# Three rows of transfers ahead of the first norm's power, first queries on GpSimd, and experts' weights by DMA

## The chip, the cores and the metric

The kernel runs on one core of one Trainium2 chip. The metric is the device time of one execution in microseconds (us), less is better. All data is float32; large products go through TensorE as float32r parts, a high one and a low one, so that the sum keeps float32's precision.

## The reference

There are 16 images of 192 channels and 32 x 32 pixels. Three stages follow each other.

```python
x = conv_attention(x)                 # whole-image norm, per-head 1x1 and depthwise 3x3 convolutions to q, k, v,
                                      # softmax over channels, output product, residual
t = to_tokens(x)                      # 1024 tokens of 192 channels per image
t = t + causal_attention(norm(t))     # 6 heads of 32 channels, then W_proj applied twice
t = t + experts(norm(t))              # softmax gate over 4 experts, the best 2 of 4 for each token,
                                      # gelu(x @ w1[e] + b1[e]) @ w2[e] + b2[e], hidden size 768
```

In the reference the causal attention works on each image's 1024 tokens as one sequence, and each expert's answer is weighted by the token's share of the two chosen gates.

## The kernel before, in words

The kernel has two parts. The first is a loop over the images, with everything but the experts. The second is a loop over 67 blocks of 512 tokens that belong to one expert each, the experts' stage.

**An image.** TensorE makes the convolutions (`conv`, L1612), mixes the channels, and builds the image's tokens in eight chunks of 128: `input_and_first_heads(k)` (L1674) and `last_heads(k)` (L1686). VectorE takes each chunk to `t_sb` (L1004) and gathers its statistics (L964 to L971). For each half of four chunks the variances are raised to the power -1/2 by GpSimd (`token_rstd`, L695; the operation is L698), VectorE writes the normed rows `xhat` (L980), TensorE transposes them (L1696), ScalarE takes the high part and VectorE the low part (L988, L991), and TensorE makes queries, keys and values (L1713, L1721). Queries and keys are then copied inside SBUF into stacks of three parts, `QS` and `KS`, by DMAs (`load_keys`, L343; `load_queries`, L348), in three waves by token: 0 to 255, 256 to 511, 512 to 1023, and two halves j of the heads each. SP issues all keys, the queries of wave 2, and of wave 0 the half j = 0; GpSimd issues the rest of waves 0 and 1. Scores (L1752, L1754), maxima (L1010), exponentials (L1451), transposes (L1764) and products with the values (L1786, L1796) follow for 48 units. After each chunk of queries VectorE inverts the sums, GpSimd spreads them over the heads' channels (`inverse_wide`, L705; L710 and L711), and TensorE transposes that (`norms`, L1800; L1804), so that the results can be scaled.

**What GpSimd does in an image, in this order.** Every engine runs its own list of instructions in order. GpSimd's is: unpad the image (L309); send the rows of the image before; the two powers of the first norm between the sends; queries of waves 0 and 1 (`load_queries`, run at L743 to L749); two additions of the output's bias (`output_bias`, L729); and eight times the spreading of the inverse sums, with the other small powers. `send(i, first, end)` (L714) issues, for each chunk of 128 tokens (a row of the loop over k), two indirect DMAs (L723), one per chosen expert, that scatter the chunk's normed tokens to the experts' blocks in DRAM (`routed_rows`). Image 0 has nothing to send. SP waits for all sends of the image before (L551) ahead of the queries of wave 2.

**The experts' stage.** `w_all` holds all experts' weights in SBUF, high and low part. For block r GpSimd copies the expert's first layer, 128 partitions x 3072 elements, to the buffer `cur[r % 2]` in eight copies (`copy_weights`, L767; L770), two after each of the first four low parts of the block before, and the biases to `bcur` (L773). The expert's number is read from a table on the chip (`tab`). TensorE transposes the block's tokens (L1925) and runs six steps: an up product of five matmuls with `cur` (`up`, L1938; L1949), one step ahead, and a down product with `g_hi` (L1965) and `g_lo` (L1970). The first up product of a block waits for `cur_sb` (L1943). ScalarE applies gelu twice, VectorE makes the low part (L1338). SP loads the next tokens (`load_block`, L576) and stores the answers (`store_block`, L583) to DRAM. When an image's blocks are all answered, a unit of 512 tokens is fetched back by eight indirect DMAs on GpSimd (`fetch`, L779; L790), which stand between the weight copies; VectorE adds them with their shares (L1374), TensorE transposes the result (L1934), and SP stores it. There are 32 such units; `UNIT_OF` gives the block in which each is finished.

## Time and profile before

| what | value |
|---|---|
| median of 3 runs | 3534.71 us (3533.25 to 3537.79) |
| profiled execution | 3531.58 us |
| its span, first to last instruction | 3529.7 us |
| TensorE matmul busy | 3125.3 us (89%) |
| VectorE busy | 2337.5 us (66%) |
| ScalarE busy | 1836.2 us (52%) |
| GpSimd busy | 1145.8 us (32%) |
| mean granted TensorE clock | 0.959 of full speed |
| DMA | 414.50 MB, mean 117 GB/s |

PE is TensorE's matmul, PEld its weight load, DVE VectorE, ACT ScalarE, POOL GpSimd, SP the engine that issues most DMAs (SPq is its queue of DMA issues). L12 is line 12 of the kernel before. A line of a timeline gives the start and the duration in us, the engine, the line and operation, and in brackets how long the engine idled before it and what ended that. "issue" is idle time that ended with nothing the profile shows. Consecutive instructions of one kind stand in one line, with their count behind the x. The granted clock is a share of 2.4 GHz: 1.00 is 2.4 GHz, 0.50 is 1.2 GHz.

### The profile page before, as it was taken

How to read it: one execution, taken by the hardware profiler on the slowest of the kernel's cores; microseconds unless marked ns; L12 is line 12 of the kernel's file. 1: busy time of each engine (PE TensorE's matmuls, PEld its weight loads, DVE VectorE, ACT ScalarE, POOL GpSimd, SP SyncE). 2: the span in 40 equal slices, each digit the busy share in tenths (PEclk: the TensorE clock that was granted, in tenths of full speed). 3: DMA queues.
4: the chain of work that ended last, by engine and by line, in shares of the span. 5: the costliest groups of instructions: out<-in, count | busy, mean ns of one | idle time of the engine just before them, and what ended most of it. 6: DMA issues, size and time to landing. Idle time of an engine off the chain costs nothing. (4 is left out here: it accounts for less than half of the span.)

```text
span 3529.7 us, 73345 instructions
## 1 busy us (share of the span) xinstructions
PE 3125.3 (89%) x26642; PEld 2381.5 (67%) x26642; DVE 2337.5 (66%) x5867; ACT 1836.2 (52%) x3868; POOL 1145.8 (32%) x1702
## 2 busy tenths in 40 slices
PE   4899898898998989989889899866999999999995
PEld 1666666566666666666656666645888888888884
DVE  3767777677676776776767767683565665665654
ACT  0547456365474563644636547443555555555553
POOL 2131312303213133031230321303454545545554
PEclk9999999999999999999999999987999999999997
DMA  7545445444364453534644445402233333333332
GB/s 175 134 112 157 108 123 144 116 133 119 111 170 109 117 138 110 150 101 124 158 112 120 126 112 163 138 21 60 82 109 102 115 96 116 103 106 110 109 104 88
DMA packets 243804, 414.50 MB, mean 117 GB/s; under 512 B 69847, under 2 KB 156311, under 8 KB 242377
## 3 DMA queue, kind: packets, MB, share of 16 engines
q1 hardware_dynamic: 207854, 343.47, 35.9%
q0 software_dynamic: 31488, 64.53, 6.4%
q8 instruction: 217, 3.56, 0.4%
q10 hardware_dynamic: 4107, 1.81, 0.3%
q14 instruction: 138, 1.13, 0.1%
HBM read 242.82 MB, written 117.71 MB: 102 GB/s over the span
## 5 line engine op out<-in xcount | busy, mean ns | idle before, releaser
L1010 DVE TENSOR_REDUCE minus_max<-ps 128x1 f32<-128x128 f32 (+7 forms) x768 | 570.6, 749 | 228.1 <-PE ps L1754 224.3
L1451 ACT ACTIVATE p_sb<-ps,minus_max 128x128 f32<-128x128 f32 (+7 forms) x768 | 567.6, 742 | 94.0 <-DVE minus_max L1010 91.2
L1764 PE MATMUL ps<-ident,p_sb 128*128 128x128 f32 x3456 | 542.6, 282 | 42.7 <-ACT p_sb L1451 17.8
L1338 DVE TENSOR_TENSOR g_lo<-g,g_hi 128x512 fp32r<-128x512 f32 x402 | 312.5, 777 | 327.6 <-ACT g_hi L1575 327.6
L1574 ACT ACTIVATE g<-ps,bcur 128x512 f32<-128x512 f32 x402 | 276.8, 689 | 466.6 <-PE ps L1949 466.6
L1752 PE MATMUL ps<-KS,QS 96*128 96x512 f32 (+3 forms) x1152 | 404.2, 410 | 56.4 <-ACT p_sb L1451 40.5
L1764 PEld LDWEIGHTS ps<-ident,p_sb 128*128 128x128 f32 x3456 | 376.0, 143 | 96.3 <-issue 33.5
L710 POOL COPY inverse_wide<-inverse_sums 128x192 f32<-128x192 f32 x128 | 44.7, 349 | 1214.5 <-DVE inverse_sums L1031 1214.5
L1965 PE MATMUL ps<-w_all,g_hi 128*128 x1608 | 436.5, 353 | 0.0
L1465 ACT ACTIVATE PT<-ps 128x512 f32<-128x512 f32 (+3 forms) x640 | 340.8, 532 | 159.7 <-PE ps L1764 151.7
L770 POOL CAST cur<-w_all 128x384 fp32r x536 | 281.2, 557 | 392.6 <-DVE g_lo L1338 392.3
L723 POOL DMA_INDIRECT routed_rows<-xhat,slot x256 | 253.1, 989 | 372.1 <-issue 372.1
L1629 PE MATMUL ps<-ring,wconv 125*32 125x512 f32 (+1 forms) x3072 | 357.1, 605 | 18.1 <-DMA ring<-padded_scratch 18.1
L790 POOL DMA_INDIRECT got<-expert_rows,slot x256 | 254.4, 994 | 154.5 <-issue 84.8
L1949 PE MATMUL ps<-X_hi,cur 128*128 128x512 f32 x804 | 263.6, 409 | 43.1 <-issue 38.9
L1970 PE MATMUL ps<-w_all,g_lo 128*128 x1608 | 294.3, 265 | 0.0
L1023 DVE COPY PT<-ps 128x512 f32<-128x512 f32 (+3 forms) x512 | 246.7, 482 | 71.7 <-PE ps L1764 71.0
L1970 PEld LDWEIGHTS ps<-w_all,g_lo 128*128 128x128 f32 x1608 | 287.5, 189 | 4.8
L1965 PEld LDWEIGHTS ps<-w_all,g_hi 128*128 128x128 f32 x1608 | 264.9, 191 | 23.2
L1752 PEld LDWEIGHTS ps<-KS,QS 96*128 96x128 f32 x1152 | 203.0, 200 | 108.7 <-ACT p_sb L1451 60.2
L1575 ACT ACTIVATE g_hi<-ps,bcur 128x512 fp32r<-128x512 f32 x402 | 273.5, 680 | 0.0
L1949 PE MATMUL ps<-X,cur 128*128 128x512 f32 x804 | 250.9, 394 | 0.0
(279 smaller groups left out, 5663.1 us busy)
## 6 DMA issues: line engine op xcount, KB each, us to landing
ring<-padded_scratch SPq DMA_DIRECT2D x576, 204.0 KB
routed_rows<-zero_rows SPq DMA_DIRECT2D x67, 384.0 KB, 5.1
xgt<-routed_rows SPq DMA_DIRECT2D x67, 384.0 KB, 4.0
expert_rows<-y_rows SPq DMA_DIRECT2D x67, 384.0 KB, 2.6
padded_scratch<-xpad SPq DMA_DIRECT2D x32, 435.0 KB, 3.5
x_sb<-x SPq DMA_DIRECT2D x16, 768.0 KB
KS<-QKh SPq DMA_DIRECT2D x128, 96.0 KB, 2.5
KS<-QKh SPq DMA_DIRECT2D x64, 192.0 KB, 3.5
```

Source lines behind the costliest of these rows:

```text
L770: g.tensor_copy(cur[r % 2][:, part], w_all[:, bass.ds(expert, 1), part].rearrange("p e f -> p (e f)")).then_inc(cur_sb, 1)
L1010: v.tensor_reduce(nmx[:, qc, h:h + 1], score_place(n), AX, ALU.max, negate=True).then_inc(mx_sb, 1)
L1338: v.tensor_tensor(g_lo[:, n % 2, :], g32[:, n % 2, :], g_hi[:, n % 2, :].bitcast(F32), ALU.subtract).then_inc(lo_sb, 1)
L1451: a.activation(p_sb[n % NP][:, 0:P * (qc + 1)], score_place(n), ACT.Exp, bias=nmx[:, qc, h:h + 1], accum_out=ls[:, qc, h:h + 1]).then_inc( ...
L1465: a.activation(PT[h][:, k0:k0 + nb, :], bank(pass_bank(t))[:, 0:P * nb].rearrange("p (k q) -> p k q", q=P), ACT.Copy).then_inc(PT_act, 1)
L1574: a.activation(g32[:, n % 2, :], bank(n % 2), ACT.Gelu, bias=b1)
L1629: last = t.matmul(bank(2 * (r % 2) + nh)[W * j:W * (j + 1), :], wconv[s][0:KROWS[s], h, c0:c0 + W], rhs, start=s == 0, stop=s == 1, skip_g ...
L1752: t.matmul(o[:, k0:k0 + keys], QS[0:96, qc // TPC, h, P * (qc % TPC):P * (qc % TPC + 1)], KS[0:96, h, k0:k0 + keys], start=True, stop=k0 + ...
L1764: last = t.transpose(bank(pass_bank(piece))[:, P * k:P * (k + 1)], p_sb[n % NP][:, P * (k0 + k):P * (k0 + k + 1)], ident[:, :])
L1949: last = t.matmul(bank(n % 2), w[:, W1L * part + P * j:W1L * part + P * (j + 1)], act_part[:, :], start=m == 0, stop=m == 4)
L1965: t.matmul(bank(acc_bank(r, tt))[:, 0:2 * C], g_hi[:, n % 2, P * tt:P * (tt + 1)], w2j, start=j == 0, stop=False, skip_group_check=True)
L1970: last = t.matmul(bank(acc_bank(r, tt))[:, 0:C], g_lo[:, n % 2, P * tt:P * (tt + 1)], w2j[:, 0:C], start=False, stop=j == J - 1, skip_grou ...
```

## The change

On GpSimd, the sends ahead of the first power are those of three chunks (six DMAs) in place of five (ten), then two chunks' between the powers, one after the second power, and the last two chunks' (four DMAs) behind the queries of wave 0. GpSimd also issues the three query DMAs of wave 0, j = 0, that SP issued. On TensorE, `last_heads(2)` and `last_heads(3)` come ahead of `input_and_first_heads(5)`.

In the experts' stage the eight copies on GpSimd go. In their place SP issues one DMA per block from `w_all` to `cur` (`load_weights`): block 0's ahead of its wait for the sends, block r + 1's at the start of its pass r, after a wait for `up_ps`, which says that block r - 1's up products have read the same buffer. The biases are still copied by GpSimd, and the eight fetches of a unit are issued in one run, at GpSimd's pass r for a unit that is finished in block r + 2.

```diff
--- before.py
+++ after.py
@@ -286,10 +286,11 @@
         STACK_LOADS = 16 * 3
         SENT = 16 * 2 * NC
 
-        cur_sb, bcur_sb, xT_ps, xT_hi, xT_lo, up_ps, gelu_sb, lo_sb, down_ps, acc_ps, y_acc, yrow_sb = sems(
-            "cur_sb bcur_sb xT_ps xT_hi xT_lo up_ps gelu_sb lo_sb down_ps acc_ps y_acc yrow_sb")
+        bcur_sb, xT_ps, xT_hi, xT_lo, up_ps, gelu_sb, lo_sb, down_ps, acc_ps, y_acc, yrow_sb = sems(
+            "bcur_sb xT_ps xT_hi xT_lo up_ps gelu_sb lo_sb down_ps acc_ps y_acc yrow_sb")
         outT_ps, outs_sb, comb = sems("outT_ps outs_sb comb")
         xgt_ld = [sem(f"xgt_ld{n}") for n in range(3)]
+        cur_ld = [sem(f"cur_ld{n}") for n in range(2)]
         yrow_st = [sem(f"yrow_st{n}") for n in range(2)]
         got_ld = [sem(f"got_ld{n}") for n in range(2)]
         tt_ld = [sem(f"tt_ld{n}") for n in range(2)]
@@ -533,12 +534,9 @@
                 for j in range(2):
                     load_keys(sp, 0, j, 0, QKh)
                     load_keys(sp, 0, j, 1, QKh)
-                load_queries(sp, 0, 0, 0, QKh)
-                load_queries(sp, 0, 0, 2, QKh)
                 sp.wait_ge(qk_lo, NQ * i + PAIR_GROUPS)
                 for j in range(2):
                     load_keys(sp, 0, j, 2, QKl)
-                load_queries(sp, 0, 0, 1, QKl)
                 for j in range(2):
                     for r, part in enumerate((QKh, QKh, QKl)):
                         load_keys(sp, 1, j, r, part)
@@ -573,6 +571,13 @@
             sp.dma_start(tokens[B - 1], t_sb[:, :, 0:C]).then_inc(t_st, 16)
 
 
+            def load_weights(r):
+                expert = sp.value_load(tab[0:1, r:r + 1], min_val=0, max_val=E - 1)
+                if r >= 2:
+                    sp.wait_ge(up_ps, J * (r - 1))
+                sp.dma_start(cur[r % 2][:, :].bitcast(F32), w_all[:, bass.ds(expert, 1), 0:4 * W1L].rearrange("p e f -> p (e f)").bitcast(F32)
+                             ).then_inc(cur_ld[r % 2], 16)
+
             def load_block(r):
                 if r >= 3:
                     sp.wait_ge(xT_ps, 2 * (r - 2))
@@ -603,10 +608,15 @@
                 sp.dma_start(o_img[P:C, :], outs_b[u % 2][:, :]).then_inc(out_st[u % 2], 16)
 
             sp.wait_ge(t_st, 16 * B)
+            sp.wait_ge(w_split, 1)
+            sp.wait_ge(table_sb, 1)
+            load_weights(0)
             sp.wait_ge(sent, SENT * B)
             for r in range(3):
                 load_block(r)
             for r in range(NBLK):
+                if r + 1 < NBLK:
+                    load_weights(r + 1)
                 if r + 1 in UNIT_OF:
                     load_tokens(UNIT_OF[r + 1])
                 if r:
@@ -732,18 +742,22 @@
             for i in range(B):
                 unpad_image(pool, i)
                 if i:
-                    send(i - 1, 0, 5)
+                    send(i - 1, 0, 3)
                 token_rstd(i, 0)
                 if i:
-                    send(i - 1, 5, 7)
+                    send(i - 1, 3, 5)
                 token_rstd(i, 1)
                 if i:
-                    send(i - 1, 7, NC)
+                    send(i - 1, 5, 6)
                 pool.wait_ge(qk_hi, NQ * i + PAIR_GROUPS)
-                load_queries(g, 0, 1, 0, QKh)
-                load_queries(g, 0, 1, 2, QKh)
+                for j in range(2):
+                    load_queries(g, 0, j, 0, QKh)
+                    load_queries(g, 0, j, 2, QKh)
                 pool.wait_ge(qk_lo, NQ * i + PAIR_GROUPS)
-                load_queries(g, 0, 1, 1, QKl)
+                for j in range(2):
+                    load_queries(g, 0, j, 1, QKl)
+                if i:
+                    send(i - 1, 6, NC)
                 for j in range(2):
                     for r, part in enumerate((QKh, QKl, QKh)):
                         load_queries(g, 1, j, r, part)
@@ -764,19 +778,14 @@
             pool.wait_ge(t_st, 16 * B)
             pool.wait_ge(table_sb, 1)
 
-            def copy_weights(r, expert, parts):
-                for n in parts:
-                    part = slice(W1L // 2 * n, W1L // 2 * (n + 1))
-                    g.tensor_copy(cur[r % 2][:, part], w_all[:, bass.ds(expert, 1), part].rearrange("p e f -> p (e f)")
-                                  ).then_inc(cur_sb, 1)
-
-            def copy_biases(r, expert):
+            def copy_biases(r):
+                expert = pool.value_load(tab[0:1, r:r + 1], min_val=0, max_val=E - 1)
                 if r >= 2:
                     pool.wait_ge(yrow_sb, 2 * (r - 1))
                 g.tensor_copy(bcur[r % 2][:, :], wb_all[:, bass.ds(expert, 1), :].rearrange("p e f -> p (e f)")
                               ).then_inc(bcur_sb, 1)
 
-            def fetch(u, chunks):
+            def fetch(u):
 
                 i, c = UNITS[u]
                 last = last_opened(i)
@@ -784,37 +793,22 @@
                     pool.wait_ge(yrow_st[n], 16 * ((last + 2 - n) // 2))
                 if u >= 2:
                     pool.wait_ge(comb, 2 * TPC * (u - 1))
-                for kk in chunks:
+                for kk in range(TPC):
                     for a in range(2):
                         col = NC * i + TPC * c + kk
                         g.indirect_dma_start(got[u % 2][:, kk, a, :], None, answers[0:BANK * (last + 1), :],
                                              bass.IndirectOffsetOnAxis(ap=slot[:, a, col:col + 1], axis=0)
                                              ).then_inc(got_ld[u % 2], 16)
 
-            expert = pool.value_load(tab[0:1, 0:1], min_val=0, max_val=E - 1)
-            copy_weights(0, expert, range(8))
-            copy_biases(0, expert)
-            for r in range(NBLK - 1):
-                expert = pool.value_load(tab[0:1, r + 1:r + 2], min_val=0, max_val=E - 1)
-                pool.wait_ge(lo_sb, J * r + 1)
-                copy_weights(r + 1, expert, (0, 1))
-                if r + 1 in UNIT_OF:
-                    fetch(UNIT_OF[r + 1], (2,))
-                pool.wait_ge(lo_sb, J * r + 2)
-                copy_weights(r + 1, expert, (2, 3))
-                copy_biases(r + 1, expert)
-                if r + 1 in UNIT_OF:
-                    fetch(UNIT_OF[r + 1], (3,))
-                pool.wait_ge(lo_sb, J * r + 3)
-                copy_weights(r + 1, expert, (4, 5))
-                pool.wait_ge(lo_sb, J * r + 4)
-                copy_weights(r + 1, expert, (6, 7))
+            copy_biases(0)
+            for r in range(NBLK):
+                if r + 1 < NBLK:
+                    copy_biases(r + 1)
                 if r + 2 in UNIT_OF:
-                    fetch(UNIT_OF[r + 2], (0, 1))
-            assert not {NBLK, NBLK + 1} & set(UNIT_OF)
+                    fetch(UNIT_OF[r + 2])
             for u in range(len(UNITS)):
                 if finish_block(u) >= NBLK + 2:
-                    fetch(u, range(TPC))
+                    fetch(u)
 
 
         @block.vector
@@ -1852,10 +1846,10 @@
                 mixing(i, 1)
                 input_and_first_heads(i, 4)
                 pe.wait_ge(mix_sb, 2 * i + 2)
-                last_heads(i, 0)
-                last_heads(i, 1)
+                for k in range(4):
+                    last_heads(i, k)
                 input_and_first_heads(i, 5)
-                for k in range(2, 6):
+                for k in range(4, 6):
                     last_heads(i, k)
                 for k in (6, 7):
                     pe.wait_ge(y_sb, NC * i + k - 5)
@@ -1940,7 +1934,7 @@
                 if n >= 2:
                     pe.wait_ge(gelu_sb, n - 1)
                 if j == 0:
-                    pe.wait_ge(cur_sb, 8 * (r + 1))
+                    pe.wait_ge(cur_ld[r % 2], 16 * (r // 2 + 1))
                     pe.wait_ge(xT_hi, 2 * (r + 1))
                     pe.wait_ge(xT_lo, 2 * (r + 1))
                 w = cur[r % 2]
```

## Rows read from the trace of the kernel before

**Rows 1.** Waits, whole span: engine and line <- releaser: us in total, times, longest.

```profile
PE ps L1949 <- issue: 38.9, 23, 2.1
DVE xhat L980 <- POOL rstd L698: 73.6, 19, 5.6
```

**Rows 2.** Windows, images 0 and 7: us; PE, PEld, DVE, ACT, POOL busy; clock; DMA.

```profile
106.00:112.00 6.00, 3.38 (x17) 2.15 (x16) 5.30 (x18) 1.20 (x3) 0.36 (x1) 1.00 0.00 0
1107.00:1113.00 6.00, 5.79 (x17) 4.23 (x18) 4.87 (x16) 1.79 (x3) 3.93 (x4) 0.50 0.19 66
```

**Rows 3.** GpSimd's timeline in image 7; then two lines' durations, min/median/max ns.

```profile
1096.85 0.96 POOL L723 DMA_INDIRECT routed_rows<-xhat,slot  x1 [0.30 <-issue]
1101.02 0.96 POOL L723 DMA_INDIRECT routed_rows<-xhat,slot  x1 [1.95 <-issue]
1104.54 1.05 POOL L698 TENSOR_TENSOR rstd<-rstd,minus_half 128x4 f32<-128x4 f32 x1
1111.83 1.04 POOL L698 TENSOR_TENSOR rstd<-rstd,minus_half 128x4 f32<-128x4 f32 x1 [1.21 <-DVE rstd L971]
1120.88 3.72 POOL L729 TENSOR_TENSOR t_sb<-t_sb,bproj_bc 128x784 f32<-128x784 f32 x2
1131.02 0.34 POOL L710 COPY inverse_wide<-inverse_sums 128x192 f32<-128x192 f32 x1 [6.42 <-DVE inverse_sums L1031]
L723 POOL DMA_INDIRECT routed_rows<-xhat,slot x256: 954/961/1135, 233.8 to 2407.9; - x128
L351 POOL DMA_DIRECT2D QS<-QKh x96: 545/547/817, 115.0 to 2261.3; - x96
```

**Rows 4.** VectorE's timeline in image 7: start us, us, operation [idle before <-releaser].

```profile
1098.27 0.36 DVE L1004 TENSOR_TENSOR t_sb<-ps,bf_bc 128x196 f32<-128x196 f32 x1 [0.74 <-PE ps L1687]
1100.21 0.17 DVE L971 TENSOR_SCALAR rstd<-tmv 128x4 f32<-128x4 f32 x1
1105.69 1.47 DVE L980 TENSOR_SCALAR xhat<-t_sb,tmv,rstd 128x192 f32<-128x192 f32 x4 [4.65 <-POOL rstd L698]
```

**Rows 5.** TensorE's timeline in image 7.

```profile
1101.33 0.49 PE L1687 MATMUL ps<-mix,vp 128*128 128x196 f32 x2
1107.21 1.97 PE L1696 MATMUL ps<-ident,xhat 128*128 128x128 f32 x8 [5.38 <-DVE xhat L980]
1118.70 0.47 PE L1713 MATMUL ps<-T,wqkv_b_hi 128*128 128x512 f32 x1 [0.32 <-DVE T L991]
1125.46 0.30 PE L1752 MATMUL ps<-KS,QS 96*128 96x128 f32 x1 [0.43 <-DMA QS<-QKl]
1131.59 0.44 PE L1804 MATMUL ps<-ident,inverse_wide 128*128 128x128 f32 x2 [0.22 <-POOL inverse_wide L711]
```

**Rows 6.** Timeline of image 0: VectorE, then TensorE.

```profile
106.46 1.25 DVE L980 TENSOR_SCALAR xhat<-t_sb,tmv,rstd 128x192 f32<-128x192 f32 x4 [0.58 <-POOL rstd L698]
117.86 0.47 PE L1713 MATMUL ps<-T,wqkv_b_hi 128*128 128x512 f32 x1 [0.32 <-DVE T L991]
```

**Rows 7.** Timeline and one window of the experts' stage; the first is its start.

```profile
2414.47 1.09 PE L1925 MATMUL ps<-ident,xgt 128*128 128x128 f32 x4 [38.23 <-DMA xgt<-routed_rows]
2536.19 0.61 PE L1949 MATMUL ps<-X,cur 128*128 128x512 f32 x2
2525.40:2540.06 14.66, 14.66 (x88) 13.29 (x88) 7.60 (x18) 8.60 (x15) 8.00 (x13) 1.00 0.38 111
2552.03 2.31 POOL L770 CAST cur<-w_all 128x384 fp32r x4
2554.45 0.69 PE L1949 MATMUL ps<-X_hi,cur 128*128 128x512 f32 x2 [1.83 <-issue]
```

**Rows 8.** DMA issues: queue, count, KB each, median us from issue to landing.

```profile
w_raw<-w_a SPq DMA_DIRECT2D x1, 1536.0 KB, 9.8
KS<-QKh SPq DMA_DIRECT2D x128, 96.0 KB, 2.5
KS<-QKh SPq DMA_DIRECT2D x64, 192.0 KB, 3.5
```

## The prediction

> **What bounds the kernel now.** I read the list of waits first, then the windows, then the order of time around two stalls. TensorE is the engine that is busy most of the time, so I look for the places where it stands still at the same point again and again. There are two. In the list of waits [rows 1] VectorE waited 73.6 us, in 19 waits, for GpSimd's power (L698), and TensorE waited 38.9 us, in 23 waits, before an up product (L1949) for something that the view does not name.
>
> First place, image 7 (its rows stand for the 15 images that have sends; the power comes at the same point in each). GpSimd issues ten indirect sends, and only then the first power, at 1104.54 [rows 3]. What the power needs, the variances (L971), was there at 1100.21 + 0.17 = 1100.4 [rows 4]. VectorE therefore idled 4.65 us and wrote the normed rows from 1105.69 on, and TensorE idled 5.38 us before its transposes at 1107.21 [rows 4, 5]. After that idle the granted clock was 0.50, the 1.2 GHz level, for six microseconds [rows 2]. Image 0 has no sends and shows the same stretch without the stall: clock 1.00 [rows 2], and from the first normed rows to the matmul after the last low part 117.86 - 106.46 = 11.4 us [rows 6], where image 7 took 1118.70 - 1105.69 = 13.0 [rows 4, 5].
>
> Second place, the experts' stage. TensorE's up product at 2554.45 came after 1.83 us of idleness, and GpSimd's last weight copies ended at 2552.03 + 2.31 = 2554.34 [rows 7]. They were late because indirect fetches stand between the copies on GpSimd. So the unnamed wait is the one for `cur_sb`.
>
> **The change, part by part.**
> 1. *Three rows (six DMAs) ahead of the first power in place of five (ten).* The sixth send ends at 1096.85 + 0.96 = 1097.8 [rows 3]. The power then waits for VectorE and no longer for sends.
> 2. *last_heads(2) and (3) ahead of input_and_first_heads(5).* VectorE waited 0.74 us for just these [rows 4]; the variances come at 1099.5 + 0.17. The later tokens don't come later. With a power of 1.04 and two hand-overs of 0.10 (1104.54 + 1.05 to 1105.69) the normed rows start at 1100.9: 4.8 us earlier. TensorE's token work ends at 1101.8 [rows 5], so its idle time shrinks to some 0.6. Image 0, where it was busy for only 3.38 of the six microseconds, kept clock 1.00 [rows 2], so I let the slow clock go too: 13.0 - 11.4 = 1.6 more. TensorE would start the scores 6.4 us earlier, at 1119.1 in place of 1125.46 [rows 5].
> 3. *First queries.* Three query DMAs leave SP's queue, three more come onto GpSimd's, 0.547 each [rows 3]. SP's keys follow sooner. TensorE's wait there, 0.43 [rows 5], goes or stays; I take nothing.
> 4. *The last two rows (four DMAs) behind the first queries, ahead of the second ones.* Nobody waits for the sends themselves until the last queries on SP, so this is free for them. But what is queued behind them is: the second queries, two additions (L729, 3.72 us) and the spreading of the sums (L710, L711) that TensorE needs for norms. GpSimd's list from 1100.8 on is ten sends of 0.96 + 0.30 = 12.6, a power of 1.04, twelve query DMAs = 6.6, the additions 3.7, hand-overs 0.5, in sum 24.4: free at 1125.2. The eighth send shows a gap of 1.95 in place of 0.30 [rows 3]; none, one or two such gaps of 1.65 can fall in. Spreading takes 0.6, so the sums are ready between 1125.8 and 1129.1. TensorE used them at 1131.59 [rows 5] and would want them at 1131.59 - 6.4 = 1125.2. So GpSimd sets the end of this stretch: the gain is 1131.59 - 1125.8 = 5.8 at best and 1131.59 - 1129.1 = 2.5 at worst. I take one gap, 4.1 us, since the pauses before the powers cover some. What is late next is thus the first norms. Over 15 images: 62 us (37 to 87). Image 0 I take at nothing.
> 5. *Weights by one DMA per block on SP.* GpSimd's copies go, and with them the 38.9 us [rows 1]. That other work hides nothing here: in these waits TensorE had nothing else. In place comes a transfer of 128 x 3072 x 4 bytes = 1536 KB. For block r + 1, SP issues it once block r - 1 has its last up product, which frees the buffer: for the block that runs from 2540.06 that product ends at 2536.19 + 0.61 = 2536.8, and the next weights are wanted where TensorE began to wait, 2554.45 - 1.83 = 2552.6 [rows 7]. The window is 15.8 us, where a block without a stall takes 14.66 [rows 7]. The price is not in the trace. From below: 1536 KB from memory landed in 9.8 [rows 8]. From above: key loads inside SBUF took 2.5 for 96 KB and 3.5 for 192 KB, so 1.0 per 96 KB, and 3.5 + 14 x 1.0 = 17.5 [rows 8]. I take 10, the row of the same size. Behind it on SP's queue stand the answers' stores and the next tokens. With 10 the weights are in at 2546.8, 6.8 into the block, and the store, issued at 2.4, some 1 later. The fetches, now 8 in a run of 8 x 1.26 + 1.65 = 11.7, end 20 into the block, landed at 22; the first sum that needs them stands in the last step of the next block, 14.66 + 12.5 = 27 in. So 5 us of room, which hides this reordering, and which a landing of 15 would use up. First block: its transposes waited for token rows until 2414.47 [rows 7], and SP sends for the weights ahead of that wait: nothing. Sum: 39, from 20 if half the blocks with fetches stay late, to 42.
>
> Here the Trainium skill has two rules, and the sum above needs neither. The page "SBUF — State Buffer", section "SBUF: two separate sides", says that a DMA from GpSimd's queue is starved of descriptors while VectorE runs a copy-like operation through both its ports, and advises SP's queue instead; that speaks against part 3. It is a rival below. The page "DMA: Bandwidth & Descriptors", section "Anatomy of one DMA", gives 2.0 us + bytes / 436 GB/s; as an estimate that is 5.6 us for the weights, and the sum would stay the same, with more room.
>
> **The sum.** 62 + 39 = 101 us. Against the profiled execution, 3531.6 us (span 3529.7 with 1.9 around it), 3431; the median of the runs is 3.1 above that execution, so 3434 us.
>
> **The rivals.**
> - *GpSimd's queue keeps most of the first gain* (chance 0.14). For it: twelve DMAs and four sends ahead of the additions; against it: the bounds of part 4. With 2 us per image the time is 3534.7 - 30 - 39 = 3466.
> - *GpSimd's issues grow beside VectorE* (0.05). For it: the longest send took 1.135 against a median of 0.961, the longest query DMA 0.817 against 0.547 [rows 3]; against it: these are rare. If all were so long, 10 x 0.17 + 12 x 0.27 = 4.9 per image, 4.1 turns into -0.8, and the time is 3534.7 + 12 - 39 = 3508. This is what the rule of the State Buffer page would do here; the medians so far speak against it.
> - *The stalls in the experts' stage were not the copies'* (0.07), but the fetches' answers', and stay: 3534.7 - 62 = 3473. Against it stand the 0.11 us between the copy's end and the up product. That is also how the change could fail to do what it says.
> - *The weights land late, and the kernel gets slower* (0.07, of which 0.02 end level). In every block TensorE waits at its last step for 17.5 - 15.8 = 1.7 us or more; the transfer shares the engines with stores, gathers and loads. The cost is 66 x 1.7 = 112 at the upper bound alone, above the 101 saved: 3534.7 - 101 + 112 = 3546, and with 1 us of sharing more 3612. It decides from 101 / 66 = 1.5 us of lateness, a landing after 17.3 us.
> - *GpSimd gets through early* (0.09): no gap, 5.8 per image: 3534.7 - 87 - 42 = 3406.
>
> **The numbers.** The forecast has 0.58, at 3434, with its own range of 3415 to 3455. The range that should hold 8 in 10 takes in the bounds of part 4 and of part 5 together: 3534.7 - 87 - 42 = 3406 and 3534.7 - 37 - 20 = 3478; I give 3404 to 3480. A measurement of this kernel tells about 0.2%, 7 us, from no change. Only late weights give a slower kernel, 0.05, or a level one, 0.02; faster 0.93.
>
> **What would show it.** The wait of VectorE for the power (73.6) should be near 0, the clock 1.00 in the six microseconds after the first transposes, TensorE's first norms should wait 0.6 to 4 us for L711 in each image, and the period of an image should be 4 us shorter. In the experts' stage the 38.9 us should be gone, a block should take 14.7 us whether it has fetches or not, and the weights should land in 6 to 12 us. I am wrong if TensorE's wait before L1949 is named as one for this DMA in most blocks, or if the wait for L711 exceeds 4 us.

## The result and the profile after

The kernel after takes 3497.39 us (median of 4 runs, 3495.86 to 3499.04), the kernel before on the same chip 3536.25 (3533.25 to 3541.68). The ratio is 0.9888, with a 95% interval of 0.9871 to 0.9906. So it is 39 us faster, where 101 were forecast, and it lies outside the range. The profiled execution took 3495.86 us, with a span of 3493.3.

In `kernel.py` after, line numbers have shifted: the first norm's power is L708, sends are L733, the spreading of the sums is L720 and L721, and a block's weight transfer is L578. I read the list of waits first, for those that answer to [rows 1]:

```profile
PE ps L1798 <- POOL inverse_wide L721: 82.0, 18, 6.5
POOL QS L352 <- issue: 43.1, 32, 2.7
PE ps L1919 <- DMA xgt<-routed_rows: 40.5, 1, 40.5
DVE xhat L974 <- POOL rstd L708: 20.8, 31, 0.8
```

Both waits on which the prediction rested are gone or small. VectorE's wait for the power fell from 73.6 to 20.8, now 0.8 at most, and the unnamed 38.9 before the up product left 0.2. But the first line is new: TensorE waits 82.0 us for GpSimd's spreading of the inverse sums, 5.1 in image 7. And the second line is GpSimd's own: it stands still 43.1 us ahead of query transfers, released by nothing that the profile shows. In the kernel before these two waits were:

```profile
PE ps L1804 <- POOL inverse_wide L711: 15.4, 26, 0.9
POOL QS L351 <- issue: 0.4, 2, 0.2
```

GpSimd's timeline of image 7 shows where its time goes (start, duration, operation, idle before and its releaser). This image's sends begin at 1083.30; in the kernel before they began at 1090.22, so subtract 6.92 from the rows of before to set them side by side.

```profile
1093.02 1.04 POOL L708 TENSOR_TENSOR rstd<-rstd,minus_half 128x4 f32<-128x4 f32 x1 [2.28 <-DVE rstd L965]
1097.25 0.96 POOL L733 DMA_INDIRECT routed_rows<-xhat,slot  x1 [1.95 <-issue]
...
1106.27 1.08 POOL L352 DMA_DIRECT2D QS<-QKh  x2 [0.65 <-issue]
1107.34 1.09 POOL L352 DMA_DIRECT2D QS<-QKl  x2
1108.73 1.03 POOL L733 DMA_INDIRECT routed_rows<-xhat,slot  x1 [0.30 <-issue]
...
1117.54 0.55 POOL L352 DMA_DIRECT2D QS<-QKh  x1 [2.26 <-issue]
...
1119.19 3.63 POOL L739 TENSOR_TENSOR t_sb<-t_sb,bproj_bc 128x784 f32<-128x784 f32 x2
1122.76 0.34 POOL L720 COPY inverse_wide<-inverse_sums 128x192 f32<-128x192 f32 x1
1123.05 0.23 POOL L721 COPY inverse_wide<-inverse_sums 128x64 f32<-128x64 f32 x1
```

The power comes early and waits for VectorE, as the change wants it. From there on, apart from the usual 0.19 to 0.30 us around a send, the list is idle only in three pauses with no releaser: 1.95, 0.65 and 2.26 us. The sums had long been ready: L720 follows the additions without a gap, where before it idled 6.42 us [rows 3]. TensorE's timeline, to compare with [rows 5]:

```profile
1112.36 0.24 PE L1746 MATMUL ps<-KS,QS 96*128 96x128 f32 x1
...
1123.34 0.69 PE L1798 MATMUL ps<-ident,inverse_wide 128*128 128x128 f32 x2 [5.13 <-POOL inverse_wide L721]
...
1132.69 0.44 PE L1798 MATMUL ps<-ident,inverse_wide 128*128 128x128 f32 x2
```

The second norms of the kernel before are this row:

```profile
1138.54 0.44 PE L1804 MATMUL ps<-ident,inverse_wide 128*128 128x128 f32 x2 [0.85 <-POOL inverse_wide L711]
```

From the start of the sends, the scores begin after 29.06 us, before after 35.24: 6.2 us won. The clock is 1.00 in the six microseconds after the first transposes, where the kernel before had 0.50 [rows 2]:

```profile
1095.70:1101.70 6.00, 4.97 (x23) 3.57 (x24) 4.87 (x15) 2.28 (x4) 3.83 (x4) 1.00 0.19 66
```

At the first norms 1.3 us are left (40.04 against 41.37), the rest went into the wait. At the second norms the kernel after is 1.1 us behind (49.39 against 48.32). Between the two norms it needs 9.35 us for what took 6.95, and the next windows say why (us; PE, PEld, DVE, ACT, POOL busy; granted clock, DMA share, GB/s):

```profile
1118.00:1123.30 5.30, 0.20 (x4) 0.00 (x0) 1.00 (x3) 0.32 (x2) 5.27 (x7) 0.83 1.04 237
1123.30:1131.00 7.70, 7.66 (x41) 5.12 (x42) 4.34 (x11) 3.96 (x14) 0.00 (x0) 0.50 0.95 278
1131.00:1139.00 8.00, 7.48 (x75) 5.46 (x75) 6.73 (x19) 5.82 (x17) 0.53 (x2) 0.95 0.02 5
```

TensorE stood idle for 5.1 us, and then worked 7.7 us at a granted clock of 0.50, the 1.2 GHz level. The kernel before had such a stretch behind the power in every image with sends [rows 2]; the change moved it from there to the first norms. Over 14 images, from the first send of one to that of the 15th, the period is 143.2 us (227.62 to 2232.37) against 142.7 before (233.84 to 2231.71). The images' part gave nothing.

The experts' stage gave nearly all of it. From the first up product to the end of the span it took 3529.7 - 2419.6 = 1110.1 us before, and 3493.3 - 2416.5 = 1076.8 after: 33 us of the 36 by which the spans differ. The weights by the DMA view, then a window of the stage, then two rows of TensorE at the start of an early block, without fetches:

```profile
cur<-w_all SPq DMA_DIRECT2D x67, 1536.0 KB, 7.1
```

```profile
2440.00:3460.00 1020.00, 1002.47 (x5877) 895.05 (x5876) 581.22 (x1292) 589.89 (x977) 270.99 (x306) 1.00 0.67 205
```

```profile
2464.96 0.36 PE L1964 MATMUL ps<-w_all,g_lo 128*128 x2
2465.58 0.73 PE L1943 MATMUL ps<-X_hi,cur 128*128 128x512 f32 x2 [0.25 <-ACT g_hi L1569]
```

The weights land 7.1 us after their issue, so in time. But the first up product of a block starts 0.26 us after the last down product has ended, released on paper by a ScalarE result that had long been there; this happens twice per block in the early ones, 0.49 us in sum, so these take 15.13 us instead of 14.66 [rows 7]. One block of the profiled execution took 21.5 us, where the others of its kind take 15.8. The last of a unit's eight fetches was issued only after 7.21 us of idleness on GpSimd, and VectorE and then TensorE waited for it:

```profile
2813.79 0.94 POOL L799 DMA_INDIRECT got<-expert_rows,slot  x1 [7.21 <-issue]
2823.10 0.44 PE L1959 MATMUL ps<-w_all,g_hi 128*128 x1 [3.41 <-DVE y_rows L1356]
```

The traces of queries_on_sp and six_behind have one such block each, that of ffn_only has none. But a pause ahead of the eighth fetch stands in all units: 3.9 to 9.4 us in 30 of the 32 here, 2.2 to 3.3 in the kernel before. The fetch ahead of it was issued at 2805.62 and landed 7.6 us later, and the eighth started at 2813.79, 0.59 us behind that. A fetch lands 5.1 us after its issue in the median, 2.7 in the kernel before.

### The profile page after: what moved, and what is told of

Its sections match the earlier page's. It is cut to its first block and busy times, and to the rows that moved or that the text cites. A ratio compares the mean times of both kernels' runs of the same rounds, so it can differ in the third digit from the quotient of the medians.

```text
span 3493.3 us, 72548 instructions
## 1 busy us (share of the span) xinstructions
PE 3130.1 (90%) x26642; PEld 2382.5 (68%) x26642; DVE 2281.9 (65%) x5867; ACT 1835.9 (53%) x3868; POOL 894.2 (26%) x1214
## 5 line engine op out<-in xcount | busy, mean ns | idle before, releaser
L1758 PE MATMUL ps<-ident,p_sb 128*128 128x128 f32 x3456 | 553.6, 286 | 43.0 <-ACT p_sb L1445 16.7
L1332 DVE TENSOR_TENSOR g_lo<-g,g_hi 128x512 fp32r<-128x512 f32 x402 | 282.6, 703 | 370.5 <-ACT g_hi L1569 370.5
L1758 PEld LDWEIGHTS ps<-ident,p_sb 128*128 128x128 f32 x3456 | 384.1, 146 | 95.9 <-ACT p_sb L1445 32.8
L1746 PE MATMUL ps<-KS,QS 96*128 96x512 f32 (+3 forms) x1152 | 414.1, 418 | 35.8 <-ACT p_sb L1445 34.9
L1623 PE MATMUL ps<-ring,wconv 125*32 125x512 f32 (+1 forms) x3072 | 356.2, 603 | 15.8 <-DMA ring<-padded_scratch 15.8
L733 POOL DMA_INDIRECT routed_rows<-xhat,slot x256 | 253.3, 989 | 373.8 <-issue 373.8
L720 POOL COPY inverse_wide<-inverse_sums 128x192 f32<-128x192 f32 x128 | 44.7, 349 | 1130.3 <-DVE inverse_sums L1025 1130.3
L1623 PEld LDWEIGHTS ps<-ring,wconv 125*32 125x32 f32 (+1 forms) x3072 | 92.9, 111 | 207.1 <-issue 191.9
```

The costliest lines, as they stand in the source:

```text
L1332: v.tensor_tensor(g_lo[:, n % 2, :], g32[:, n % 2, :], g_hi[:, n % 2, :].bitcast(F32), ALU.subtract).then_inc(lo_sb, 1)
L1623: last = t.matmul(bank(2 * (r % 2) + nh)[W * j:W * (j + 1), :], wconv[s][0:KROWS[s], h, c0:c0 + W], rhs, start=s == 0, stop=s == 1, skip_g ...
L1746: t.matmul(o[:, k0:k0 + keys], QS[0:96, qc // TPC, h, P * (qc % TPC):P * (qc % TPC + 1)], KS[0:96, h, k0:k0 + keys], start=True, stop=k0 + ...
L1758: last = t.transpose(bank(pass_bank(piece))[:, P * k:P * (k + 1)], p_sb[n % NP][:, P * (k0 + k):P * (k0 + k + 1)], ident[:, :])
```

## The experiments

Each ratio is against the kernel before on the same chip. A difference between two kernels that ran on different chips carries the 1 to 3 us by which the kernel before differs there (3536.25, 3537.41, 3538.93 and 3538.78 us). First I split the change.

**image_only**: the kernel before with the images' part of the change; the weights' part left out. 

> The change's image part alone (sends, first queries, order of the tokens); the experts' stage as before. Theory A (the wait moved from the first power to the first spreading of the sums, and the slow clock with it): the kernel is within 5 us of the kernel before, TensorE waits about 5 us for the spread sums in each of 15 images. Theory B (the image part does gain, and the new weight transfers lose it again in the experts' stage): 3475 us or less.

**ffn_only**: the reverse. 

> The change's experts' part alone (weights by one DMA per block); the image loop as before. Theory A: all of the gain is here, 3498 to 3503 us. Theory B: 3530 us or more.

Measured: image_only 3534.96 us (ratio 0.9997, 0.9983 to 1.0011); ffn_only 3500.03 (0.9905, 0.9881 to 0.9929). The waits of image_only, then of ffn_only:

```profile
PE ps L1805 <- POOL inverse_wide L708: 80.1, 20, 6.3
PE ps L1950 <- issue: 41.7, 24, 2.1
```

```profile
PE ps L1689 <- DVE xhat L973: 84.1, 16, 6.5
```

So the weights' part brings 37 us (3537.41 - 3500.03), and the images' part nothing clear of the noise: one wait replaced another of the same size. That the second causes the loss was still an argument. It was tested by taking the four late sends out of GpSimd's way.

**sends_behind_sums**: the kernel after, with

```diff
                 for j in range(2):
                     load_queries(g, 0, j, 1, QKl)
-                if i:
-                    send(i - 1, 6, NC)
...
                     inverse_wide(i, qc)
+                    if i and qc == 0:
+                        send(i - 1, 6, NC)
```

> The whole change, with the last two rows' sends (four DMAs) moved once more, behind the first spreading of the sums. Theory A: GpSimd's list ahead of the sums is shorter by four sends and a gap, 5.1 + 2 us, so TensorE's wait of 5 us and the slow clock after it go, and 15 images gain 5 to 6 us each: 3407 to 3425 us. Theory C (the first key and query transfers, not GpSimd's list, hold the scores back): within 10 us of the changed kernel.

**queries_on_sp**: the kernel after, with the three moved query transfers back on SP, at their old place among the keys, and GpSimd's as before:

```diff
-                for j in range(2):
-                    load_queries(g, 0, j, 0, QKh)
-                    load_queries(g, 0, j, 2, QKh)
+                load_queries(g, 0, 1, 0, QKh)
+                load_queries(g, 0, 1, 2, QKh)
                 pool.wait_ge(qk_lo, NQ * i + PAIR_GROUPS)
-                for j in range(2):
-                    load_queries(g, 0, j, 1, QKl)
+                load_queries(g, 0, 1, 1, QKl)
```

> The whole change, but the three first-query DMAs stay on SP's queue. Theory A: GpSimd's list is shorter by 3 x 0.55 us and at most one pause of 0.65, so the wait for the sums is 5.1 - 2 = 3 us; the clock may or may not fall after 3 us of idleness: 3440 (clock kept) to 3467 us (clock lost). If GpSimd's queries were slowed beside VectorE, the gain would be larger still. Theory C: no gain, or a loss through SP's later keys.

Measured: sends_behind_sums 3391.98 us (0.9588, 0.9572 to 0.9604), queries_on_sp 3445.18 (0.9718, 0.968 to 0.9756). The wait, in each in turn:

```profile
PE ps L1798 <- POOL inverse_wide L721: 17.0, 34, 0.9
```

```profile
PE ps L1799 <- POOL inverse_wide L724: 30.9, 21, 2.4
```

With the sends out of the way the 82 us are 17, and 105 us go, more than the wait itself held, and more than the 3407 to 3425 us that I had expected. In image 7 the first norms come 34.6 us after the sends began instead of 40.0, and the second 6.95 behind them instead of 9.35. The windows of image 7 of sends_behind_sums around its first norms, at 1082.2, show what came on top:

```profile
1080.00:1085.00 5.00, 4.52 (x36) 2.94 (x36) 4.01 (x12) 4.19 (x18) 2.60 (x5) 1.00 0.76 174
1085.00:1092.00 7.00, 5.97 (x61) 4.21 (x60) 6.51 (x17) 4.76 (x15) 2.42 (x4) 1.00 0.41 102
```

The clock stays at 1.00. In queries_on_sp TensorE waits only 1.52 us for the sums in image 7 (2.4 is its longest of all images), and the clock still falls to 0.50:

```profile
1112.00:1118.00 6.00, 6.00 (x35) 3.87 (x35) 3.74 (x10) 2.44 (x9) 0.20 (x1) 0.50 1.08 278
```

In images 8 and 10 of the same trace it stays at 1.00 behind waits of 1.73 and 1.33 us. So the time lies in the range that I had expected, but not by its working: the wait is 1.5 us in place of 3, and the clock is lost in most images. The four runs of queries_on_sp lie between 3422.70 and 3449.58 us, the shortest with a mean granted clock of 0.974, the others with 0.964 to 0.966.

This run also says what the queries' move does in the kernel after: with the three transfers back on SP it is 52 us faster. The images' part without that move gives 55 us (3500.03 - 3445.18), of the 62 that were forecast with it.

Next the single parts, and the half microsecond in the experts' blocks.

**order_only**: the kernel before with TensorE's token order alone.

```diff
-                last_heads(i, 0)
-                last_heads(i, 1)
+                for k in range(4):
+                    last_heads(i, k)
                 input_and_first_heads(i, 5)
-                for k in range(2, 6):
+                for k in range(4, 6):
```

> The kernel before with TensorE's order alone: the four tokens' groups ahead of the last input's group, sends and queries as before. The prediction took nothing for this. Theory A (all of the images' part hangs on when GpSimd has the first sums): the power stays behind the ten sends, so 3537 us within 6. Rival: the order itself costs or gives something, because the last input's first heads come later (the first norm's input is ready earlier but nothing takes it): 16 x 1.5 = 24 us later, 3561 us.

**queries_only**: the kernel before with the queries' move alone, the diff of queries_on_sp read the other way. 

> The kernel before with the three first-query transfers moved from SyncE to GpSimd, sends and TensorE's order as before. In the kernel before TensorE waited 15.4 us in 26 waits for the first sums, at most 0.9 us: GpSimd had no room left. Theory A with the new price (a transfer into the queries is issued by GpSimd in 0.65 to 2.3 us of its sequence where the prediction took next to nothing): the first sums come 2 to 4 us later in each of 15 images, and the slow clock behind the idle stretch adds 0 to 2: 3537 + 30 to 90, 3567 to 3627 us, with TensorE's wait for inverse_wide at 45 to 100 us. Rival (the prediction's step 3, that these issues lie behind the power and take nothing): 3537 within 6.

**sums_queries_sp**: sends_behind_sums with the diff of queries_on_sp. 

> The kernel of sends_behind_sums with the three first-query transfers back on SyncE. In sends_behind_sums TensorE waits 17.0 us in 34 waits for the first sums, 0.9 at most, and GpSimd waits 2.6 us for VectorE's sums: GpSimd is off the path. Theory A: the place of the queries is worth nothing once GpSimd has room, 3392 us within 6. Rival: the queries on GpSimd cost by themselves (they land later than SyncE's would, so the first scores are late), and going back gives what queries_on_sp gave over the kernel after, some 50 us: 3340 us. Third: SyncE's queue is late with the keys when it carries the queries too, some 1 us an image: 3407 us.

Measured: order_only 3539.88 (1.0002, 0.9988 to 1.0015), as expected nothing. The other two were misses, on the same point: queries_only 3500.61 (0.99, 0.9881 to 0.9919), 38 us faster where I had expected 30 to 90 slower, and sums_queries_sp 3425.29 (0.9683, 0.9665 to 0.9701), 33 slower than sends_behind_sums where I had expected nothing. The prediction's step 3 had taken nothing for the queries as well. SP's queue shows it, the kernel before first, then queries_only:

```profile
1118.23 1.25 SPq L351 DMA_DIRECT2D QS<-QKh  x2
1119.53 2.71 SPq L345 DMA_DIRECT2D KS<-QKl  x2
1122.28 1.01 SPq L351 DMA_DIRECT2D QS<-QKl  x1
```

```profile
1093.81 2.30 POOL L351 DMA_DIRECT2D QS<-QKh  x4
1096.09 1.09 POOL L351 DMA_DIRECT2D QS<-QKl  x2
```

Before, the last of the first queries is issued by SP at 1122.28, 32.1 us after the image's sends began (1090.22), behind two key transfers of 1.36 us of issue each; the scores at +35.24 wait for just this one (0.43, `QS<-QKl`, [rows 5]; 14.6 us in 16 waits over the whole span, none in queries_only). In queries_only GpSimd has issued it by 1097.18, 28.5 us after its sends began (1068.70), and the scores start at +33.25. So the move is worth 2 us an image, the image's period is 140.7 instead of 142.7, and it comes out only where GpSimd has room for it. The expectation's step that failed is the direction: I priced what three more issues cost GpSimd and not what they free on SP. In queries_only they cost no time, since the ten sends keep the scores late enough, and the first norms wait 0.21 us. In sums_queries_sp TensorE waits for SP's last query in every image, 1.05 us in image 7, and the clock falls behind that, so more is lost than the wait. The wait over the whole span, then the window behind it in image 7:

```profile
PE ps L1747 <- DMA QS<-QKl: 19.6, 16, 1.7
```

```profile
1094.00:1100.50 6.50, 6.49 (x36) 4.55 (x36) 4.20 (x13) 4.24 (x18) 2.83 (x5) 0.50 0.80 178
```

**sums_and_table**: sends_behind_sums, and the number of the next block's expert is read by TensorE in the middle of the block before.

```diff
                 if j == 0:
-                    expert = pe.value_load(tab[0:1, r:r + 1], min_val=0, max_val=E - 1)
+                    expert = coming if r else pe.value_load(tab[0:1, 0:1], min_val=0, max_val=E - 1)
...
+                if j == 2 and r + 1 < NBLK:
+                    coming = pe.value_load(tab[0:1, r + 1:r + 2], min_val=0, max_val=E - 1)
```

> The kernel of sends_behind_sums, and TensorE reads the next block's entry of the table in the middle of the block before instead of at its first up product. In the kernel after, the first up product of each block came 0.24 to 0.30 us late twice (some 0.49 us a block), with the wait put down to ScalarE's g_hi, which had long been done. Theory D: TensorE's own read of the table entry is what is late, since it now runs beside a transfer of 1536 KB. Then the blocks without fetches go from 15.13 back to 14.65 us, 67 x 0.1 to 0.49 = 7 to 33 us off at most, some 8 to 12 likely since only the early blocks show it: 3380 to 3385 us. Rival: the weight loads or the products themselves are slowed by the transfer's writes, and the read hides: 3392 us as sends_behind_sums, blocks at 15.13.

Measured: 3371.14 us (0.9539, 0.9515 to 0.9562), 21 below sends_behind_sums, more than the likely value and within the bounds. By the traces the experts' stage gave 14 of them, from the first up product to the end: 3368.4 - 2310.1 = 1058.3 us against 3394.5 - 2321.8 = 1072.7. The rest lies ahead of that stage, and nothing here explains it. TensorE's row at the same point of a block:

```profile
2357.02 0.37 PE L1964 MATMUL ps<-w_all,g_lo 128*128 x2
2357.22 0.65 PE L1943 MATMUL ps<-X_hi,cur 128*128 128x512 f32 x2
```

The gap is gone, and every block but the first that has no output transposes, with fetches in it or not, takes 14.62 to 14.66 us, while the weights are transferred exactly as before. So it was the read, not the transfer's writes. That the read is slow because of the transfer beside it is likely (in the kernel before it cost nothing that showed: 14.66), but no run had the transfer without the read at its old place and another source.

At last the dose: how many sends stand ahead of the sums.

**two_behind**: the kernel after, with the last row's two sends behind the first sums, in the manner of sends_behind_sums. 

> The kernel after with two of GpSimd's four late transfers (the last row's) moved behind the first sums, where sends_behind_sums moved all four. In image 7 of the kernel after TensorE waits 5.1 us for the first sums, and the granted clock is 0.50 for some 10 us from 1121.3; in queries_on_sp it waits 2.4 us and the clock is still 0.50 for 7 us; in sends_behind_sums it waits 0.9 at most and the clock stays at 1.00. Two transfers take 2.5 us of GpSimd. Theory E (the time of the wait and a clock price that comes whole with any such wait): the wait goes to 2.6 us and the clock still falls, so 15 x 2.5 = 38 us of the 105 go, 3460 us (3450 to 3475), and the other 67 lie in the last two transfers. Rival (the gain is in proportion to the wait alone): half of it, 3445 us within 8. Third: GpSimd's own pause of 2.3 us moves out of the way with the two transfers: the wait is gone, 3395 to 3410 us.

**six_behind**: sums_and_table with six sends there: `send(i - 1, 5, 6)` dropped, `send(i - 1, 5, NC)` behind the first sums. 

> The kernel of sums_and_table (3371 us) with six transfers behind the first sums instead of four, ten ahead. TensorE's waits for GpSimd there are 17 us in 34 waits for inverse_wide, 0.9 at most, and VectorE's for the second power is short. Theory A (what GpSimd has ahead of the sums matters only while TensorE waits for it): nothing is left to take, 3371 us within 6. Rival one: the two transfers still delay the second half's norm or the queries, 1 us in each of 15 images, 3356 us. Rival two: six transfers in a row after the first sums hold back the second sums, 7 us later, by 1 to 3 us an image: 3386 to 3416 us.

Measured: two_behind 3425.83 us (0.9679, 0.9647 to 0.9711), six_behind 3427.67 (0.9681, 0.9648 to 0.9713). Neither fits its likeliest theory. Two sends give 72 us of the 105, more than their share and less than all; six are 57 us worse than four. For six_behind rival one had forecast a gain, and rival two had the right sign with too small a price. Its waits, and GpSimd's timeline of one image:

```profile
PE ps L1796 <- POOL inverse_wide L721: 35.8, 33, 2.1
PE ps L1688 <- DVE xhat L972: 21.7, 17, 2.0
```

```profile
1201.71 1.07 POOL L733 DMA_INDIRECT routed_rows<-xhat,slot  x1 [16.84 <-issue]
1206.31 0.96 POOL L733 DMA_INDIRECT routed_rows<-xhat,slot  x1 [3.54 <-issue]
...
1217.87 0.95 POOL L733 DMA_INDIRECT routed_rows<-xhat,slot  x1 [1.96 <-issue]
```

TensorE waits 2.1 us for the second spreading in every image, where sends_behind_sums has 0.85: that is rival two's mechanism, 1.2 us an image. Much of the rest goes with the pauses, which have moved and grown: 3.54 and 1.96 among the sends here, and the scores start 29.90 us after the sends began, against 28.51 in image 7 of sends_behind_sums. One block of the experts' stage took 21.2 us as well. Summed over the 15 images (pauses over 0.45 us ahead of a send or a query, from the first send on), GpSimd paused 2.1 us an image in the kernel before, 5.2 in the kernel after, 4.2 in two_behind, 3.5 in sends_behind_sums and 6.3 in six_behind. Where the traces tell the landings of single sends, they also tell what a pause waits for. The seventh send of image 7 in the kernel before was issued at 1098.12, the eighth at 1101.02 [rows 3], and the seventh landed between them, 2.32 us after its issue (the view rounds it):

```profile
DMA to landing us min/median/max: 2.3/2.3/2.3
```

The eighth follows 0.59 us behind that landing, and so it is with all 17 such pauses in each of the kernel before, ffn_only, order_only and queries_only, the long ones (2.89 us) included. Sends elsewhere follow each other at 1.26 us, ahead of the landing. Of the 16 long pauses ahead of a query transfer in queries_only, 12 end 0.36 us after the landing of the fifth transfer before it. So moving a transfer on this queue moves the pauses too, and a price per transfer alone is not enough. Theory E of two_behind assumed a wait of 2.6 us with the clock at 0.50 behind it; the whole wait for the sums is 27.6 us in 26 waits there, 1.9 at most, so less than E needs. The clock does not hang on this wait alone either: in image 8 (first norms at 1230.05) it is only 0.29 us, and yet the clock falls, ahead of it already:

```profile
1222.00:1229.00 7.00, 6.08 (x40) 4.40 (x40) 4.24 (x14) 5.01 (x23) 6.49 (x8) 0.77 1.00 249
1230.00:1233.00 3.00, 2.96 (x13) 2.39 (x14) 1.87 (x5) 2.19 (x8) 2.04 (x2) 0.57 0.14 44
```

The table holds the kernels that differ in GpSimd's list. The period is the mean of 14 images, from the first send of the first to that of the 15th; the wait is TensorE's for the spreading.

| kernel | sends ahead of the first power / of the sums | first queries | period, us | wait, us |
|---|---|---|---|---|
| before | 10 / 16 | SP and GpSimd | 142.7 | 15.4 |
| queries_only | 10 / 16 | GpSimd | 140.7 | 16.9 |
| after | 6 / 16 | GpSimd | 143.2 | 82.0 |
| queries_on_sp | 6 / 16 | SP and GpSimd | 139.2 | 30.9 |
| two_behind | 6 / 14 | GpSimd | 138.1 | 27.6 |
| six_behind | 6 / 10 | GpSimd | 138.8 | 35.8 |
| sums_queries_sp | 6 / 12 | SP and GpSimd | 137.8 | 13.8 |
| sends_behind_sums | 6 / 12 | GpSimd | 135.8 | 17.0 |

Alone, the earlier power gives 3.5 us an image, and the moved queries 2. Together, with all sends ahead of the sums, they give nothing, because GpSimd's list is full and each fills it further: beside the earlier power the queries' move costs 4.0 us an image (143.2 against 139.2). With four sends taken off that list they give 6.9.

## Why the prediction was wrong

Step 1, the first power no longer behind sends: right. It waits 2.28 us for VectorE, and VectorE's wait for it is 0.8 at most.

Step 2, the order and the clock behind the first transposes: right in the main, with the scores 6.2 us earlier where 6.4 were forecast. The order alone, without the moved sends, gives nothing (order_only).

Step 3, the queries, at nothing: wrong both ways. Where GpSimd has room the move gives 2 us an image (queries_only, and sums_queries_sp against sends_behind_sums). In the kernel after GpSimd is full, and the move costs 4.0 us an image, 52 us in all (queries_on_sp). The three issues, 3 x 0.547 us, were counted in step 4's list; the pauses ahead of query transfers, 43.1 us in total against 18.7 in queries_on_sp, were not.

**Step 4 failed, and with it nearly the whole miss:** 62 us were forecast for the images, and 2 or nothing came. It named the right mechanism and "what is late next", and sized it too low, twice. First, GpSimd's list from the first power's end to the spread sums was put at 25.0 us, and up to 28.3 with two pauses of 1.65. It measured 1123.28 - 1094.06 = 29.2, of which the three pauses are 4.86, 0.30 of that the usual distance between two sends; without them it would be 24.7, as forecast. The forecast took its one kind of pause from [rows 3] and had no row for a pause ahead of a query. That made the wait 5.1 us instead of 0.6 to 4.0, over the 4 us that the prediction named as its sign of being wrong, and the first norms come 1.3 us earlier instead of 4.1. Second, it let the wait cost only its own length. The rows for the rest lay in its hands: 5.38 us of idleness with 0.50 behind them [rows 2, 5]. It counted that slow stretch as won back after the transposes, and did not count it as lost again at the new wait. That cost 2.4 us between the first norms and the second. 1.3 - 2.4 = -1.1 in image 7, and the period ended at -0.5.

The first rival, "GpSimd's queue keeps most of the first gain", is what happened, at 0.14, and its price of 2 us an image was too kind as well: nothing was left. The rival in which GpSimd's issues grow beside VectorE did not come: the medians are 0.961 us for a send and 0.547 for a query transfer, as in [rows 3]. The pauses lie between the issues. The page "SBUF — State Buffer" of the Trainium skill, section "SBUF: two separate sides", would let VectorE's copies hold back GpSimd's transfers. That does not cover all pauses. In image 3 of two_behind GpSimd paused 1.29 us ahead of a query transfer, while VectorE did nothing at all (its row, then the window with 0.00 for VectorE):

```profile
531.74 0.60 POOL L352 DMA_DIRECT2D QS<-QKh  x1 [1.29 <-issue]
```

```profile
530.50:531.70 1.20, 0.62 (x6) 0.48 (x5) 0.00 (x0) 0.57 (x2) 0.00 (x0) 1.00 0.84 260
```

What the traces show for the pauses ahead of the eighth send is the landing of the one before it. Whether VectorE lengthens others stays open.

Step 5, the weights: 37 us by ffn_only and 33 by the two traces, against 39 (20 to 42). The block of 21.5 us holds 5.7 of the difference between 39 and 33. The prediction had put a unit's fetches at 11.7 us with one pause of 1.65, and 5 us of room behind them; with pauses of 3.9 to 9.4 that room was mostly used up, and once it was not enough. The landing was 7.1 us, inside 6 to 12; it is nearer to the 5.6 that the prediction worked out, as an estimate, from the Trainium skill's rule ("DMA: Bandwidth & Descriptors", "Anatomy of one DMA") than to the 10 that I took from a load out of memory, and the estimate is 1.5 us short. The Trainium skill fits that rule to DMAs that GpSimd issues, which the prediction left out; this one is issued by SP. That a block takes 14.7 us with or without fetches was wrong, though not for the fetches. Early blocks took 15.13, for the table read, which I had not priced; and a block with eight output transposes takes 15.8, since these are matmuls of TensorE's own:

```profile
2494.07:2508.73 14.66, 14.66 (x88) 13.25 (x87) 8.23 (x18) 8.59 (x15) 7.54 (x8) 1.00 0.77 228
2508.73:2524.55 15.82, 15.73 (x96) 13.92 (x95) 10.20 (x24) 9.54 (x17) 2.25 (x3) 1.00 0.79 234
```

These are two blocks of sums_and_table, 88 and 96 matmuls, TensorE busy in both nearly throughout. The first has fetches in it and takes 14.66 us, so the fetches themselves cost nothing there.

The sum as it came out: 37 + 2 (ffn_only 37, image_only 3537.41 - 3534.96 = 2, which its interval does not tell from nothing; 3536.25 - 3497.39 = 39 for both parts) instead of 39 + 62.

## What to carry to other kernels

When work is moved along an engine's list so that something can start earlier, add up that list to the next thing somebody waits for, pauses included that the trace shows, which can be waits for a landing, and ask whether the moved work could go behind that too; here this turned 39 us into 145, and with the table read into 168. Price a new idle stretch of TensorE at its length plus the slow clock behind it. Two changes that each pay alone can cancel where both load the same queue, so measure them apart and together.

## What the runs showed of the hardware that was not expected

- GpSimd's queue pauses, and the list of waits calls it "issue". One pause of 1.94 us or more comes in every image with sends of the kernels before and after, ahead of the eighth send since the last queries. In two_behind, sends_behind_sums and six_behind, where two, four and six sends fall behind the last queries, it stands from the second such image on ahead of the sixth, fourth and second send, so at the same count; in six_behind it lasts 2.3 to 4.0 us there, and a second one of 1.96 follows seven sends later. A second kind, 0.5 to 3.1 us, comes mostly ahead of query transfers: 0.4 us in total in the kernel before and 0.6 in sums_queries_sp, with nine of them on GpSimd, but 18.7 in queries_on_sp, with nine as well, and 43.1 in the kernel after, with twelve. The pauses ahead of the eighth send end 0.59 us after the seventh has landed, and most of those ahead of a query in queries_only 0.36 us after the landing of the fifth transfer before. Why the queue waits at these places, and what the others wait for, is open.
- The same pause ahead of the eighth fetch of a unit grew from 2.2 to 3.3 us to 3.9 to 9.4 in the kernel after, where SP moves the weights in the same stage and a unit's fetches are issued in one run; a fetch's landing went from 2.7 to 5.1 us in the median.
- A wait of 1.52 us (image 7 of queries_on_sp) was followed by 6 us at a granted clock of 0.50, much as the wait of 5.13 was in the kernel after; waits of 1.73 (image 8 of the same trace) and of 0.85 (image 7 of the kernel before) were not. But behind a wait of 0.85 in image 9 of the kernel before, at 1421.87, the clock was 0.50 from 1424.0 to 1427.4, and image 8 of two_behind shows a lowered clock with a wait of only 0.29. So the length of this one wait is not the whole rule.
- TensorE's read of a table entry at the start of a block cost nothing visible in the kernel before (14.66 us a block). In the kernels with the weights' transfer, at 205 GB/s in all, it held TensorE up by some 0.5 us in early blocks, and moving it took 14 us from 67 blocks. That the transfer slows the read is likely and not shown.
